# Row maxima formed and turned within one step, and their parts and copies issued in that step

## The reference

```python
# blocks 0 and 2, on a layer norm of x, half of the result is added to x
attn = softmax(einsum("bhnd,bhmd->bhnm", q, k) / sqrt(8));  y = einsum("bhnm,bhmd->bhnd", attn, v) @ w_proj
one_hot = one_hot(argmax(y_norm @ gate_w + gate_b));  h = gelu(y_norm @ w1[e]);  out = one_hot . (h @ w2[e])
# block 1 (mid)
scores = einsum("bhqd,bhkd->bhqk", q, k) * scale + compute_bias(N, N, rel_bias_table)
attn = softmax(scores);  out = (attn @ v) @ w_proj.T + b_proj
```

## Time and profile before

| | us |
|---|---|
| median of 3 runs | 2434.37 (2427.79 to 2437.42) |
| the profiled execution | 2440.39 |
| its span, first to last instruction | 2438.6 |
| busy in the span: PE / DVE / ACT / POOL | 2145.5 / 1934.6 / 1897.4 / 769.3 |
| granted TensorE clock, mean | 0.932 |

### The profile page before, as it was taken

How to read it: one execution, slowest core, us unless ns; L and a number is a source line. 1 busy time by engine, 2 the same in 40 slices (tenths; PEclk the granted TensorE clock), 3 DMA queues, 4 the chain that set the end, 5 groups by cost and what they waited for, 6 DMA issues and landing times. The chain is left out here.

```text
span 2438.6 us, 59781 instructions
## 1 busy us (share of the span) xinstructions
PE 2145.5 (88%) x22882; PEld 768.1 (31%) x22882; DVE 1934.6 (79%) x3219; ACT 1897.4 (78%) x3553; POOL 769.3 (32%) x1167
## 2 busy tenths in 40 slices
PE   5899888889988989999999899999889888998955
PEld 2222221226422323552233223222222222542255
DVE  6989898895688897568888898899989998568410
ACT  1688798788878777788778778788979988887822
POOL 1353523430443522033333013023062132052362
PEclk7899898899989999999999999999999999998987
DMA  3224422124403334552433233111111103531365
GB/s 105 84 86 131 120 61 71 42 86 138 112 17 105 94 98 144 173 138 69 116 95 102 78 101 86 44 38 27 37 27 43 29 22 98 155 83 43 85 178 137
DMA packets 265568, 213.37 MB, mean 87 GB/s; under 512 B 64241, under 2 KB 219761, under 8 KB 265250
## 3 DMA queue, kind: packets, MB, share of 16 engines
q1 hardware_dynamic: 254018, 201.15, 29.4%
q0 software_dynamic: 11264, 8.40, 1.9%
HBM read 159.62 MB, written 59.77 MB: 90 GB/s over the span
## 5 line engine op out<-in xcount | busy, mean ns | idle before, releaser
L1309 ACT ACTIVATE probs<-psum 128x512 f32<-128x512 f32 x3072 | 1618.2, 602 | 305.3 <-PE psum L1076 189.1
L1422 DVE TENSOR_REDUCE maxes<-psum 128x2 f32<-128x1024 f32 x1216 | 1422.0, 1215 | 241.7 <-PE psum L1044 229.7
L1113 PE MATMUL psum<-probs,v_ones 128*9 128x256 f32 (+1 forms) x11520 | 992.1, 418 | 0.1
L1076 PE MATMUL psum<-q_staged,k_staged 27*128 27x512 f16 x3072 | 806.0, 404 | 52.8 <-DMA q_staged<-neg_max 21.3
L1044 PE MATMUL psum<-k_staged,q_staged 24*128 24x512 f16 x3072 | 628.7, 407 | 156.4 <-DVE maxes L1422 121.0
L1427 DVE CUSTOM_DVE_ANT_0 biased<-psum,strips 128x512 bf16<-128x512 f32 x640 | 408.5, 685 | 92.2 <-PE psum L1044 77.5
L1044 PEld LDWEIGHTS psum<-k_staged,q_staged 24*128 24x128 f16 x3072 | 145.5, 91 | 896.5 <-DVE maxes L1422 512.9
L1076 PEld LDWEIGHTS psum<-q_staged,k_staged 27*128 27x128 f16 x3072 | 222.3, 91 | 183.3 <-ACT probs L1309 88.8
L1113 PEld LDWEIGHTS psum<-probs,v_ones 128*9 128x9 f32 x11520 | 171.9, 89 | 331.3 <-issue 234.1
L825 POOL TENSOR_SCALAR max_rest<-max_turned 128x32 f32<-128x32 f32 x96 | 28.3, 295 | 654.3 <-DVE max_turned L1465 652.2
L823 POOL TENSOR_SCALAR max_rest<-max_turned,far_bias_rows 128x32 f32<-128x32 f32 x32 | 12.9, 404 | 354.3 <-DVE max_turned L1465 354.1
(11 more groups left out here) (167 smaller groups left out, 1301.6 us busy)
## 6 DMA issues: line engine op xcount, KB each, us to landing
m_w<-in_w SPq DMA_DIRECT2D x204, 256.0 KB
near<-bias_near SPq DMA_DIRECT2D x128, 160.0 KB
strips<-bias_strips SPq DMA_DIRECT2D x64, 288.0 KB, 3.1
k_staged<-k_parts SPq DMA_DIRECT2D x192, 48.0 KB
heads<-heads_t SPq DMA_DIRECT2D x384, 18.0 KB
m_y<-sorted_tokens SPq DMA_DIRECT2D x34, 192.0 KB
expert_out<-m_out SPq DMA_DIRECT2D x34, 192.0 KB
q_staged<-q_parts SPq DMA_DIRECT2D x128, 48.0 KB
```

The source lines that it names most:

```text
L1076: mm_ = pe.matmul(bank[:, :], k.kst[p][rows_, kt * P:(kt + 1) * P], queries, start=True, stop=not biased_)
L1113: last = pe.matmul(heads_bank[32 * j:32 * j + VC, columns], k.v[:, batch_of(u) * KT + kt, u % QUADS * 4 + j, :], probs[:, step % 3 * 4 + j ...
L1309: act.activation(probs[:, step % 3 * 4 + e % 4, :], bank[:, :], ACT.Exp, scale=unscale[is_mid(u)]).then_inc(taken, 1)
L1422: dve.reduce_max(maxes[u % 2][:, half, 2 * i:2 * i + 2, t, chunk], slot, AX.X).then_inc(drained, 1)
```

## The change

In `dve_step`, the combining of a half's maxima (`dve_row_max`) goes from behind the second maximum of step LAG (or LAG + KT = 11) to between the two maxima of that step, and the turning (`dve_turn`) from behind the first maximum of the next step to behind the second maximum of this one. The addition of the far bias in mid (`dve_far`) goes from step 11 to the end of step 10. POOL's `pool_parts` and SP's `carry_max` go one step ahead, from step 4 or 12 to step 3 or 11. No instruction is added or removed.

```diff
         dve_next_max(dve, u, t, 0)
-        if t == LAG + 1:
-            dve_turn(dve, u, 1)
-        if t == LAG + KT + 1 and u + 1 < UNITS:
-            dve_turn(dve, u + 1, 0)
-        if t == LAG + KT and u + 1 < UNITS:
-            dve_far(dve, u + 1)
-        dve_route(dve, u * UNIT_STEPS + t, 0)
-        dve_next_max(dve, u, t, 1)
-        dve_route(dve, u * UNIT_STEPS + t, 1)
         if t == LAG:
             dve_row_max(dve, u, 1)
         if t == LAG + KT and u + 1 < UNITS:
             dve_row_max(dve, u + 1, 0)
+        dve_route(dve, u * UNIT_STEPS + t, 0)
+        dve_next_max(dve, u, t, 1)
+        if t == LAG:
+            dve_turn(dve, u, 1)
+        if t == LAG + KT and u + 1 < UNITS:
+            dve_turn(dve, u + 1, 0)
+        dve_route(dve, u * UNIT_STEPS + t, 1)
+        if t == LAG + KT - 1 and u + 1 < UNITS:
+            dve_far(dve, u + 1)
...
-                    if t == LAG + 1:
+                    if t == LAG:
                         carry_max(sp, u, 1)
...
-                    if t == LAG + KT + 1 and u + 1 < UNITS:
+                    if t == LAG + KT and u + 1 < UNITS:
                         carry_max(sp, u + 1, 0)
                     pace(sp, step)
...
-                    if t == LAG + 1:
+                    if t == LAG:
                         pool_parts(pool, u, 1)
-                    if t == LAG + KT + 1 and u + 1 < UNITS:
+                    if t == LAG + KT and u + 1 < UNITS:
                         pool_parts(pool, u + 1, 0)
```

## The result

The changed kernel takes 2504.93 us (median of 4 runs, 2493.67 to 2506.38) against 2435.89 us for the kernel before: a ratio of 1.0269, 95% interval 1.0242 to 1.0296. That is 69 us slower, by the ratio 65 us. The forecast was slower by 23 us.

The account below looks back on a forecast made before the run. PE and DVE were taken to hold each other, no single engine being the limit. 2440.4 - 18 + 32 + 8 + 1 = 2463, forecast as 2457 us since the profiled execution is 6 us above the median; range 2431 to 2481.

Parts of the forecast that it names:

- Part 1: Turn, parts and copies come earlier, so PE's 21.3 us of waits for the copies fall to 3: 18 us gained.
- Part 2: On SP the heads' loads now stand behind the copies, so DVE waits for the sums: 32 us lost.
- part 3: PE's clock: 75 us new at 1.2 GHz behind new stalls, 48 us gone with old waits; net 27, 8 us lost.
- The nine in plain units: Sums' loads in plain units without experts' matmuls: seven waits of 1.8 us and two of 3, together 18.6 us.
- The six in mid: Sums' loads in mid without experts: 3.3 us of wait each, 20 us, of which 14 stay as loss.
- The one "in the last half of mid": A single sums' load in mid's last half, said to have time enough: nothing lost.
- Transfers of step 3 other than the heads': SP's weights and experts' tokens: delayed about as much as step 4's transfers come earlier, set at zero.
- the six heads' loads in the experts' stretches: Sums' loads where experts' matmuls run: DVE is idle for 34 of 81 us there, so nothing lost.
- Rival 5: Expert weights and tokens of step 3 come behind the copies and PE waits: 17 us more, 2474 us; chance 0.10.
- Rival 1: SP's loads of the sums land in time after all, only the gain is left: 2402 us; chance 0.08.
- rival 2: DVE's waits half fall into its idleness, or PE catches up: about 2433 us, no change; chance 0.17.
- Rival 4: PE's clock falls 10.2 us after each stall, 150 us new at the low level: 2480 us; chance 0.15.

Follow-up runs that it names:

- experiment 4: The kernel before with only the new order of DVE and POOL, SP's copies staying in steps 4 and 12: 2423.47 us, 0.9941 of the kernel before.
- experiment 1: The changed kernel with the heads' loads (sums and values) issued ahead of the copies in steps 3 and 11: 2461.45 us, 1.0078 of the kernel before.
- experiment 2: The changed kernel with the experts' transfers (weights, tokens, output store) ahead of the copies, heads' loads still behind: 2484.21 us, 1.0171 of the kernel before.
- experiments 3 and 4: Experiment 4, and the changed kernel with both heads' loads and experts' transfers ahead of the copies: 2436.55 us, 0.9977 of the kernel before.
- experiment 7: The changed kernel with DVE's reciprocal one step later (behind step 7 or 15), its store and load too: 2470.65 us, 1.0162 of the kernel before.
- experiment 5: The kernel before with only SP's copies moved to steps 3 and 11, DVE and POOL unchanged: 2554.79 us, 1.0493 of the kernel before.

## Why the prediction was wrong

The direction was right and the size was not: 23 us were forecast and 65 measured. By the forecast's own terms:

- **Part 1, the earlier turn.** Forecast 18 us of gain and some clock with it. By itself, with SP's list as before, it measured 14 us (experiment 4). PE's waits for the copies fell to 6 us where 3 were to be left. Right in kind, a little too large.
- **Part 2, the heads' loads.** Forecast 32 us, and 8 with the clock of part 3. Measured 47 us (experiment 1), so right in kind and 7 us too small. The waits themselves are 55.8 us in 16, where the forecast's raw sum was 18.6 + 1.1 + 20 = 40. All three groups were too small. The nine in plain units are 26.6 us where 19.7 were reckoned: in the second halves SP issues the sums 7.1 to 8.7 us behind the turn's end and not 6.9, and the two where SP itself is late are 3.7 and 6.0 us. The six in mid are 27.2 us where 20 were; in the three that stand behind a piece of the strips the sums take 2.5 to 3.0 us from issue to reciprocal, and 1.83 had been read where nothing large stood ahead. The one "in the last half of mid", set to nothing, waited 2.1 us.
- **Transfers of step 3 other than the heads'.** This is the step that failed: "they are delayed by about as much as those of step 4 come earlier; I set this at zero". They cost 24 us for the experts (experiment 2) and some 9 us for the rest (experiments 3 and 4), 33 of the 42 us by which the forecast was short. The exchange is not even, because the transfers of step 4 do not come earlier by it. SP is free of the copies when the parts have come and the copies have landed, 6.6 us behind the turn's end in unit 35 in both kernels, wherever SP began to wait. The turn moved by 1.2 us; the transfers of step 3, which used to go out before the wait, now go out behind it and ahead of those of step 4. In units 10 and 11 SP is in that wait for 12 us (554.0 to 565.86), the weights of step 3 come 17 us later, and the store of step 4 comes 7 us later as well (569.15 and 576.08), with 1.7 us of each due to the stretch's later start.
- **Where a delay costs.** The same zero was given to the six heads' loads in the experts' stretches, and there it was right: none of them waited. But the reason, that DVE has room there, doesn't hold for transfers that ACT and PE wait for, since PE was busy for 80.3 of 81.0 us. Rival 5 had this mechanism, with 17 us and a chance of 0.10, and its sign is in the trace: the three new waits for `m_y`. It looked for PE's waits for weights and tokens alone; there is none for the weights, those for the tokens are 7.6 us, and the larger one, ACT's for the store, it didn't name.
- **Part 3, the clock.** The new stretches behind the reciprocals were there and about as long as forecast (84 us for 75), but the time at 1.2 GHz grew by 79 us in all where 27 were forecast. How much of the 48 us went that were to go with PE's waits for the copies was not looked at; there are also new stretches that were not forecast, as between half-units 22 and 26, where the granted clock is 0.95 and was 0.99. What that costs was not measured by itself. The heads' loads gave back 47 us for 55 us of waits (experiment 1), and the later reciprocal 26 for 34 (experiment 7); these are whole times, with any cost of the clock in them. So a cost on top of the waits is not to be seen in these numbers, nor excluded, since part of the waits may fall where DVE would have been idle.

The measured terms are -14 + 47 + 24 + 9 = 66 us, against 65 by the ratio. That they meet is less of a proof than it looks: -14 and +9 are two steps of one chain and lead to 0.9977 by themselves, so what is tested is that 47 and 24 together make the 71 us from there to 1.0269. The split is also that of one order: taken the other way, SP's new place first costs 120 us (experiment 5) and the earlier turn then gives back 55. Rival 1 (the sums land in time) and rival 2 (no change) are out by the trace. Rival 4 had the clock as the cause of the excess, by stretches of 10.2 us behind each stall; the terms measured account for the excess without it, but no run here changed the clock alone.

The Trainium skill, page "TensorE: Matmul & The Clock Gate", section "Terms", puts the penalty at the throttled time times (1 - K/N); for the 79 us more at 1.2 GHz that is an estimate of 39.5 us. No run here shows whether they cost that.

## What to carry to other kernels

A wait in an engine that issues DMAs is a fence for everything behind it. What a transfer loses that is moved behind it is not the length of the copies but the time from where it used to be issued to the end of the wait (17 us for the weights at 556.04), and what already stood behind it gains only if the wait itself ends earlier. When a step is moved ahead in such a list, go through what it now stands in front of, find who consumes each of those transfers and how soon, and don't book the exchange as even. Move the producer alone first: here the earlier turn on DVE gained 0.6% with SP's list untouched. Then look for a wait that protects nothing yet: the one for the last landing was worth 0.5% in the kernel before and 0.8% with the earlier turn when it was made only where the buffer is written again. And where one engine has room, look at the others before a delay is put at nothing.

## What the runs showed that had not been expected

- Late transfers cost time even where DVE, which holds PE in most other places, has room. In the experts' stretches DVE is idle for 34 of 81 us, and yet the experts' transfers cost 24 us (experiment 2). It was ACT and PE that waited, ACT 5.48 us at once for one store of 192 KB, and PE had no room.
- A small load (32 KB of sums) takes 1.67 us from issue to use in unit 35, with nothing large just ahead of it, and 2.5 to 3.0 us in the three places of mid where one piece of 288 KB was issued 0.46 or 0.47 us ahead of it.
- Letting SP go 1.0 to 1.3 us earlier, 95 times, gave 13 us in the kernel before, 33 us in the changed one and 19 us with the earlier turn alone (0.9862 against 0.9941).
